# A three-part decoder block on one core: the memory turned by VectorE and stored in the first phase, instead of turned by TensorE in the second

## The reference, cut to what matters

```
x = x + attn(layernorm(x))             # linear attention, 16 heads, conv with 3 taps, projections Wq Wk Wv Wp
x = x + xattn(layernorm(x), ctx_1024)  # cross-attention on a memory of 512 x 512 per batch
x = x + ffn(layernorm(x))              # a gated recurrence over the 16 batches, then tanh

xattn: mn = mem * rsqrt(mean(mem^2) + 1e-6) * (1 + rms_scale)   # one factor per memory row, one per feature
       k, v = mn @ kv_w[0], mn @ kv_w[1]                        # 1 key/value head of 128
       q    = rmsnorm(x) @ q_w                                  # 4 query heads of 128
       k, q = rope(k), rope(q);  softmax(q k^T, masked) v;  @ out_w
```

## Time and profile before

| | |
|---|---|
| median of 3 runs | 3089.86 us (3088.77 to 3090.32) |
| the profiled execution | 3088.35 us |
| its span | 3086.6 us |
| granted TensorE clock, mean | 0.996 |
| PE busy | 3034.9 us, 98% |
| DVE, ACT, POOL busy | 61%, 41%, 27% |
| HBM read and written | 184.57 MB, 98.57 MB |

### The profile page before, as it was taken

One profiled execution on the slowest core, in us unless ns is written; L12 is line 12 of the kernel. 1 busy time (PEld: TensorE's weight loads), 2 busy tenths in 40 slices (PEclk: granted clock), 3 DMA queues, 4 the chain that ended last, 5 costly groups with the idle time before them and its releaser, 6 DMA issues.

```text
span 3086.6 us, 40196 instructions
## 1 busy us (share of the span) xinstructions
PE 3034.9 (98%) x15108; PEld 2557.7 (83%) x15108; DVE 1894.2 (61%) x4081; ACT 1272.5 (41%) x2419; POOL 828.9 (27%) x699
## 2 busy tenths in 40 slices
PE   8999999999889999999999989999999999999999
PEld 7888888888768888888888878888888888888887
DVE  6777777778588777877877765243233343332455
ACT  4434343434366666666666653122211221212243
POOL 0101010111146666766666650000000000000144
PEclk9999999999999999999999999999999999999999
DMA  4555555554621122212221232111211112111386
GB/s 150 140 148 139 150 137 156 131 161 126 191 78 65 61 71 82 71 56 84 69 71 56 82 110 65 59 51 52 62 41 41 41 55 55 55 28 45 138 291 225
DMA packets 232385, 300.42 MB, mean 97 GB/s; under 512 B 13056, under 2 KB 111360, under 8 KB 232192
## 3 DMA queue, kind: packets, MB, share of 16 engines
q1 hardware_dynamic: 232192, 297.85, 31.8%
HBM read 184.57 MB, written 98.57 MB: 92 GB/s over the span
## 4 chain that ended last, share of the span: by engine, by line
PE 96%; DVE 2%; issue 1%; ACT 1%; DMA 1%; POOL 0%; SPq 0%; DVEq 0%; ACTq 0%
PE c_p L131 11%; PE c_p L132 11%; PE c_p L130 11%; PE a_p L130 6%; PE a_p L132 6%; PE a_p L131 6%; PE b_n L132 5%; PE b_n L130 5%; PE b_n L131 5%; PE b_t L1663 3%; PE d_p L131 2%; PE d_p L130 2%; PE d_p L132 2%; PE a_r L130 2%; PE a_r L131 2%; PE a_r L132 2%
## 5 line engine op out<-in xcount | busy, mean ns | idle before, releaser
L1283 POOL TENSOR_SCALAR b_soft<-b_soft,b_one_in_sum 128x512 f32<-128x512 f32 x256 | 401.2, 1568 | 299.9 <-DVE b_one_in_sum L1466 299.9
L1912 ACT ACTIVATE c_gate<-c_p,c_bias 128x512 f32<-128x512 f32 x180 | 124.2, 690 | 682.6 <-PE c_p L132 682.6
L1942 DVE TENSOR_TENSOR c_gate<-c_gate,c_gate 128x512 f32<-128x512 f32 x64 | 44.2, 690 | 503.1 <-ACT c_gate L1912 503.1
L1485 DVE TENSOR_TENSOR b_p_lo<-b_t,b_p_hi 128x512 fp32r<-128x512 f32 x256 | 175.1, 684 | 159.2 <-ACT b_p_hi L1340 156.5
L1331 ACT ACTIVATE b_soft<-b_soft,b_minus_top 128x512 f32<-128x512 f32 x256 | 185.2, 724 | 180.6 <-DVE b_minus_top L1477 176.0
L351 POOL TENSOR_TENSOR kept_scale<-c_ln_ve,minus_half 128x4 f32<-128x4 f32 x16 | 16.1, 1009 | 880.0 <-DVE c_ln_ve L343 880.0
L1340 ACT ACTIVATE b_p_hi<-b_t 128x512 fp32r<-128x512 f32 x256 | 151.6, 592 | 107.9 <-PE b_t L1663 107.9
L616 ACT ACTIVATE a_elu<-a_p 128x512 f32<-128x512 f32 x128 | 75.5, 590 | 284.5 <-PE a_p L132 284.5
L351 POOL TENSOR_TENSOR a_ln_sc<-a_ln_ve,minus_half 128x4 f32<-128x4 f32 x16 | 16.3, 1018 | 627.2 <-DVE a_ln_ve L343 627.2
L1477 DVE CUSTOM_DVE_ANT_0 b_soft<-b_l,b_mask_row 128x512 f32<-128x512 f32 x256 | 175.2, 685 | 0.0
L1663 PE MATMUL b_t<-ident,b_soft 128*128 128x128 f32 x1024 | 154.8, 274 | 10.9 <-DVE b_p_lo L1485 9.8
(11 more groups left out here) (294 smaller groups left out, 9572.9 us busy)
## 6 DMA issues: line engine op xcount, KB each, us to landing
a_res<-in_x SPq DMA_DIRECT2D x16, 1024.0 KB, 6.8
a_att_shuffled<-x SPq DMA_DIRECT2D x64, 256.0 KB, 5.1
x<-a_res SPq DMA_DIRECT2D x16, 1024.0 KB, 5.2
b_mem<-in_ctx SPq DMA_DIRECT2D x16, 1024.0 KB, 5.4
b_x<-x SPq DMA_DIRECT2D x16, 1024.0 KB, 5.5
b_res<-x SPq DMA_DIRECT2D x16, 1024.0 KB, 5.5
x<-b_res SPq DMA_DIRECT2D x16, 1024.0 KB, 4.5
c_x<-x SPq DMA_DIRECT2D x16, 1024.0 KB, 5.5
```

Source lines behind the costliest of these rows:

```text
L1283: pool.tensor_scalar(soft[:, at, :], soft[:, at, :], one_in_sum[:, at:at + 1], None, ALU.mult).then_inc(p_norm.sem, p_norm.unit)
L1485: dve.tensor_tensor(part.low, pT_bank[:, :].rearrange("p (i s) -> p i s", i=T), part.high_f32(), ALU.subtract).then_inc(p_lo.sem, p_lo.unit)
L1912: act.activation(gate[j % 2][i][:, :], gating.banks[(3 * j + i) % 6][:, :], ACT.Tanh if g == "c" else ACT.Sigmoid, bias=added[:, i, j:j + ...
```

## The change

- **Phase A, every step.** The memory of the batch is loaded twice (`load_memory`, behind the stores of the step before): in token rows into `mem_turned` and shuffled into `mem_moving`. ACT squares the token rows with a sum per row (`memory_square`, behind `elu_front(3)` and ahead of `values(0)`). DVE then overwrites `mem_turned` with the turned memory (`memory_turned`, behind `weight_low(WP)`, ahead of its wait for `att_moved`). SP stores it to the scratch tensor x2 (`store_memory`).
- **To make room**, tokens and attention results are shuffled into the buffers they came from (`x`, `att`) and both go through x1.
- **Phase A's end.** The attention result of the last batch isn't sent through DRAM: PE turns it (`turn_last`), between the first products of phase B, into one PSUM bank.
- **Phase B.** `turn_memory`, `square` and `mem_apply` are gone. `load_mem` loads the turned memory, in the contiguous direction, into `memT_f`, the place of the low part. It now waits for the key/value products of `new`, and stands behind `load_x`. ACT copies the high part in slots 6 to 9, POOL subtracts the low part in slots 7 to 10. The factors of all 16 x 512 memory rows are made at once on POOL at the end of A (`mem_power`, 128x64). They are applied in `values_high` (four 128x128 copies with a scale for each half, instead of one of 128x256) and in `keys`.
- Feature order in phase B is interleaved (feature = 4 p + c), so weights are loaded as `(p c)` and x is turned with `turn_interleaved` (a step of 16 B between elements).

```diff
@@ phase A: SP, then DVE
+            def load_memory(sp, b):
+                if b >= 1:
+                    sp.wait_ge(mem_stored.sem, mem_stored.upto(b - 1))
+                self.load_shuffled(sp, mem_moving, io["ctx_1024"], b, mem_in)
+                sp.dma_start(mem_turned[:, :, :], self.token_rows(io["ctx_1024"], b)).then_inc(mem_in.sem, mem_in.unit)
+            def store_memory(sp, b):
+                sp.wait_ge(mem_squared.sem, mem_squared.upto(b))
+                sp.dma_start(self.token_rows(self.x2, b), mem_turned[:, :, :]).then_inc(mem_stored.sem, mem_stored.unit)
+            def memory_turned(dve, b):
+                dve.wait_ge(mem_sq.sem, mem_sq.upto(b))
+                for c in range(C):
+                    self.turn_squares(dve, mem_turned, mem_moving, c).then_inc(mem_squared.sem, mem_squared.unit)
...
@@ PE, called in phase B's step 0: c = 0 in slot 0, the others in slot 2
+            def turn_last(pe, c):
+                if c == 0:
+                    pe.wait_ge(*last_bank_freed)
+                    pe.wait_ge(att_sb.sem, att_sb.upto(B - 1))
+                else:
+                    pe.wait_ge(z_f.sem, z_f.upto(B - 1, c - 1))
+                self.turn_interleaved(pe, last_bank, att, c).then_inc(attT.sem, attT.unit)
...
@@ phase B: SP, ACT, POOL
             def load_mem(sp, b):
                 if b >= 1:
-                    sp.wait_ge(memT_ps.sem, memT_ps.upto(b - 1))
-                sp.dma_start(mem[:, :, :], self.token_rows(io["ctx_1024"], b)).then_inc(mem_in.sem, mem_in.unit)
+                    sp.wait_ge(kv_ps.sem, kv_ps.upto(b - 1))
+                sp.dma_start(memT_f[:, :, :], self.token_rows(self.x2, b)).then_inc(mem_in.sem, mem_in.unit)
...
+            def memory_high(act, b, c):
+                act.wait_ge(mem_in.sem, mem_in.upto(b))
+                act.activation(memT.high[:, c, :], memT_f[:, c, :], ACT.Copy).then_inc(mem_hi.sem, mem_hi.unit)
+            def memory_low(pool, b, c):
+                pool.wait_ge(mem_hi.sem, mem_hi.upto(b, c))
+                pool.tensor_tensor(memT.low[:, c, :], memT_f[:, c, :], memT[:, c, :].high_f32(), ALU.subtract).then_inc(mem_lo.sem, mem_lo.unit)
...
@@ a step of phase B on SP
                     if following(new, B):
-                        load_mem(sp, new.b + 1)
                         load_mask(sp, new.b + 1)
                         load_x(sp, new.b + 1)
+                        load_mem(sp, new.b + 1)
...
@@ on POOL
+                        if following(new, B) and 7 <= j <= 10:
+                            memory_low(pool, new.b + 1, j - 7)
...
@@ on ACT
                         if old and j < J - 2:
                             exp(old.b, j + 2)
...
-                            if 3 <= j <= 6:
-                                square(act, after, j - 3)
-                            if j == 8:
-                                mem_apply(act, after, 0)
-                                mem_apply(act, after, 1)
-                            if j == 10 or j == 11:
-                                mem_apply(act, after, j - 8)
+                        if after and 6 <= j <= 9:
+                            memory_high(act, after, j - 6)
...
@@ on PE
-                        if following(new, B) and j in (13, 14):
-                            turn_memory(pe, s, new.b + 1, 2 * (j - 13))
-                            turn_memory(pe, s, new.b + 1, 2 * (j - 13) + 1)
```

More of the change, by code:

```diff
@@ L535, in phase_a @@
             ATT, OUT = 0, GROUPS
+            last_bank, last_bank_freed = first.bank(B, 1), first.freed(B, 1)
             raw_bank = lambda i, c: second.banks[(C * i + c) % 3]
@@ L549, in step @@
                         sp.dma_start(res[:, :, :], self.token_rows(io["x"], old.b)).then_inc(res_in.sem, res_in.unit)
-                    if old:
+                    if new and old:
                         shuffle_att(sp, old.b)
@@ L565, in step @@
                         self.b_load_query_weight(sp)
+                    if new:
+                        store_memory(sp, new.b)
+                    if following(new, B):
+                        load_memory(sp, new.b + 1)
+                    if new and new.b == B - 1:
                         sp.wait_ge(kq_ps.sem, kq_ps.upto(B - 1))
                         self.b_load_memory_weight(sp)
+                        sp.wait_ge(mem_stored.sem, mem_stored.upto(B - 1))
+                        self.b_load_output_weight(sp)
                         sp.wait_ge(kv_ps.sem, kv_ps.upto(B - 1))
@@ L596, in step @@
                     if new and new.b == B - 1:
-                        self.b_mem_power(pool, 0)
+                        self.b_mem_power(pool)
+                        for c in range(C):
+                            self.b_memory_low(pool, 0, c)
                 pipeline(B, step)
@@ L647, in step @@
                         weight_high(WQ, 2)
+                        for t in range(T):
+                            memory_square(act, new.b, t)
                     for c in range(C):
@@ L682, in step @@
                             self.b_memory_weight_high(act, c)
+                        for c in range(C):
+                            self.b_memory_high(act, 0, c)
                 def tokens_high(b, c):
@@ L798, in step @@
                         weight_low(WP, 2)
+                        memory_turned(dve, new.b)
                     if old:
@@ L1012, in phase_b @@
             p = [self.split(ctx, f"b_p{i}", [P, T, S]) for i in range(2)]
-            mem = sb("mem", [P, T, D])
+            memT = Split(sb("memT_hi", [P, C, S], F32R), Place(nc, self.base + 1024 * 196).tile("b_memT_lo", [P, C, S], F32R))
+            memT_f = Place(nc, self.base + 1024 * 196).tile("b_memT_f", [P, C, S])
             rope = sb("rope", [P, 4, S])
@@ L1303, in step @@
                             query_low(old.b, 3)
-                        if j == 7 and following(new, B):
-                            mem_power(pool, new.b + 1)
                         if new:
@@ L1424, in step @@
                             tokens_high(j - 4)
-                        if after and j >= 14:
-                            memory_high(act, s, after, 2 * (j - 14))
-                            memory_high(act, s, after, 2 * (j - 14) + 1)
                         if old and j < J - 2:
@@ L1547, in step @@
                             p_low(fin.b, J - 1)
-                        if after and j == 15:
-                            memory_low(dve, s, after, 2)
-                            memory_low(dve, s, after, 3)
                         if old and j < J - 2:
@@ L1732, in step @@
                             keys_values(1)
+                            if s == 0:
+                                for c in range(1, C):
+                                    self.a_last_turn(pe, c)
                         if 3 <= j <= 6:
```

185 lines of the change are left out of this document (79 added, 106 removed).

## The result

The changed kernel takes 3196.6 us (median of four runs, 3193.1 to 3198.1), the kernel before took 3089.3 beside it: ratio 1.0345, interval 1.0328 to 1.0361. It is slower by 107 us; the forecast was 67.5 slower. The profiled execution has a span of 3194.7 us against 3086.6, +108.1.

What follows compares the result with a forecast made beforehand. PE, busy 98% of the span and all of 100 us in mid-phase B, was taken as the bound. Terms -26 - 17.5 + 90 + 21 = +67.5 on 3088.35 gave 3155.9, as a median 3157 us; range 3118 to 3182.

Steps and rivals of the forecast that it cites:

- Removed from PE: Phase B, batches 1 to 15: 60 groups of memory turns at 0.44 us each leave PE, 26 us gained.
- End of A: End of phase A: PE turns the last attention result itself, so x's turns come earlier; 17.5 us gained, ends 10 and 20.
- Late load: Phase B: memory load behind load_x stalls PE before turn_p(7), 5.9 us in steps 1 to 14, 7.5 in step 0; +90.
- Clock: Phase B, behind the stalls: most end at 1.2 GHz, 1.4 us lost each, 15 times; +21, ends 0 and 42.
- Phase A: Steps of A: DVE's four extra transposes, 4.15 us, fill its wait for the attention result; 0, at worst 31.
- Small edits and strided turns: Phase B: POOL's and ACT's edits stay off the path, at worst 15 us; 16 B turns at most 1 us; both taken 0.
- lower end of the term: Late load in phase B: if memory lands 5.4 us after its own issue, the stall is 3.7 us, all in all 55.
- uncut upper end: Whole time with the upper ends of wait and clock: 3089.9 - 36 + 100 + 42 = 3196, before cutting to 3182.
- A: Rival for phase B: only the turns count, ACT's wait for the memory is covered; 3046 us, chance 9%.
- B: Rival for phase B: the stall comes but the clock holds; 3136 us, chance 25%.
- C: Rival: VectorE becomes the bound of phase A too, as the hole closes and the 2.1 us slack is used; 3188 us, 7%.

Runs made afterwards that it cites:

- e4: e1 with two groups of four memory turns put back on PE in slot 14, into a bank nobody reads; 3079.7 us.
- e8: e1 with exp(15) behind p_high(13) on ACT and the reciprocal for tile 15 behind masked on DVE; 3076.9 us.
- e11: e8 with POOL's scale for x behind tile 0's scaling in slot 15, and DVE normalising x's first part behind p_lo(15) in slot 0; 3071.1 us.
- e2: Changed kernel with ACT's copy of the memory in slots 7 to 10 and POOL's subtraction in slots 8 to 11; 3151.9 us.
- e10: e1 with the first memory's five loads behind the second x, and POOL's bias additions at A's end behind DVE's last z_lo; 3076.2 us.
- e9: e1 with x turned in contiguous pieces instead of every fourth word, so results differ from the reference; 3075.6 us.
- e1: Changed kernel with load_mem issued ahead of load_x in phase B; 3080.4 us, ratio to before 0.9972.
- e7: Changed kernel with the products of encode(old, 0) done three times instead of once in slot 7; 3171.2 us.
- e12: e11 with the first memory's loads behind the second x, and POOL's bias additions at A's end behind DVE's normalised x; 3064.4 us, ratio to before 0.9920.

## Why the prediction was wrong in size

Direction and main mechanism were right; the time was 40 us too low and outside the range. By its own steps, in the profiled executions (the sums are over all steps of B, slot by slot against before):

| Step of the prediction | forecast | measured | from |
|---|---|---|---|
| Removed from PE | -26 | -7.7 | slots 13 to 15: 7.92 to 7.36, steps 1 to 14; no gain seen in step 0 |
| End of A | -17.5 | -13.6 | b_x issue -9.23 with +4.35 of the start in it |
| Late load | +90 | +88.9 | slot 7 of steps 1 to 14, 81.4 in sum (5.8 each), + 7.50 |
| Clock | +21 | +27.4 | slot 8 of steps 1 to 14, 26.1 in sum (1.9 each), + 1.3 in step 0 |
| Phase A | 0 | +4.4 | stores of x1 |
| Small edits and strided turns | 0 | +8.6 | slots 0 to 6: +0.57 in each of 13 steps; step 15 and behind it +1.2 |
| Sum | +67.5 | +108.0 | the spans differ by 108.1 |

**The late load: right.** Place, victim and length (5.9 and 7.5 forecast; 4.84 to 5.91, 5.6 on average, and 7.50 measured), the two issues within 0.4 us, ACT's wait of 9.4 (I said 8 to 9), PE busy for 93 of 100 (I said 91). That step 0 fits to the hundredth is luck: its own terms, 10.2 - 2.5, give 7.7. (The lower end of the term, given as 55, comes to 57 in the same way.)

**Removed from PE: the step that failed.** It said that "each operation taken from it is a gain of its length", from a PE that shows 100%. In slot 13 the turns gave 0.70 of their 0.87 us, in slot 14 nothing, and slot 15 grew by 0.15. The loop of handovers between DVE and ACT that the turns had covered holds 2.68 us a slot, and e4 shows it by putting eight turns back for nothing. Two handovers in a row bounded it: e8 cut this loop, and only with the next one cut too (e11) did the step follow PE's own work. My check of the next handover was made in slots 6 and 7 only, whereas the turns stood in 13 and 14, the two slots with the least other work. The sentence that I wrote myself there, that a full PE "says nothing about how near the other engines' handovers are", applied to the removal first of all. I also named no range for this term, so that its miss of 18.3 us, the largest of all, was outside any bound.

**The clock: right in kind, low in size.** 1.9 a stall instead of 1.4. The reason I gave for the fall, a stall "longer than 4.6", was worth nothing: in e2 it fell behind ten stalls of 1.98 to 3.77 us, and held behind three, of 2.17, 2.20 and 3.62. As I took the time at half speed (2.8 us) from one place at the end of A, so I had one sample; in the step above the clock is low from before 1260 until about 1265.8, 3.6 us after PE starts at 1262.24, and half of that is 1.8. The Trainium skill ("TensorE: Matmul & The Clock Gate", section "HAM oscillation — how this bites in real kernels") says that a wait for a DMA in each round of a loop throttles anew in each round; all 14 steps of the changed kernel agree.

**Phase A.** Its steady steps are as forecast: DVE's transposes fit into the hole and PE stays at 100. What I left out was the first step, where five DMAs stand ahead of the second x while SP's issues are slow (8.68 us for four). For B the prediction asked what stands ahead of a load in SP's list; here it did not. e10 shows it: with the five behind that load the wait is gone.

**End of A.** The chain came as told, but each low part took 1.03 to 1.38 us instead of the 0.69 that I had from a stretch in which POOL was idle. The power over 128x64 took 10.5 us (I estimated 17), hidden as expected.

**Small terms.** Strided turns at 0 were wrong by 0.23 a step (e9); 0.35 a step, most of it in slot 3, is not traced to a cause. All misses but one went the same way, which a range from single ends could not hold. The uncut upper end, 3196, meets the measured time by luck: it was made of a longer load and a dearer clock, neither of which came.

**The rivals.** A named the gain that e1 shows to be there (3080), but valued the turns at full length, 3046. B is excluded by the windows and by e7. C is excluded: phase A's steps did not grow.

## What to carry to other kernels

A load's place in its queue is set by the waits ahead of it: before moving one, write down when it is issued, when it lands, and which in-order engine asks for it first; here two lines in the other order were 116 us. Before crediting a removed operation on a full engine with its length, go to the very slots where it stands and sum the loop of handovers there without it, or look for a step of the same kernel that does without the operation, as step 15 here: the engine's idle share shows only what the removed work did not cover. And when a loop is cut and the step does not move, look for the engine that now waits longest just behind; cutting only both loops gave the 0.66 us a step.

## What was not expected of the hardware

- A stall of TensorE of 1.98 us was enough for the granted clock to fall, and one of 3.62 was not (e2: it fell in ten steps of thirteen); a stall of 5.9 filled with products kept it at 1.00 in e7's full steps. Each fall cost 1.8 us in e7's comparison of slot 8.
- VectorE slowed beside GpSimd, by operation: subtraction of two SBUF inputs 0.68 alone, 1.03 to 1.38 beside it; normalisation in place (one SBUF input, fp32) 0.48 alone, 1.19 beside it; `k_swap`, a product of two SBUF inputs of 128 columns, 0.28 alone and 1.36 to 1.38 beside it (e12). GpSimd's additions took 1.26 each alone, 1.32 to 1.59 beside these. The Trainium skill ("SBUF — State Buffer", section "Who interferes with whom") says that a VectorE instruction with two SBUF inputs contends with a GpSimd instruction that reads SBUF. The subtractions and `k_swap` agree: they lost 0.35 to 1.1 us each, the most where the operation itself is shortest. The same section says that VectorE in a two-port mode, which a tensor_scalar can enter, contends with GpSimd, and that the one that comes second is fully blocked while the other's instruction lasts. The normalisations are such operations and lost 0.7 us each on average beside additions of 1.43; whether each of them was blocked, and for how long, no run here shows.
- A weight load for a turn takes 140 ns from contiguous words (e9) and 204 with a stride of 16 B (e1, medians); of the 64 ns difference 0.23 / 16 = 14 ns a turn showed in the step.
- SyncE's issues took 8.68 us for four DMAs of 256 KB while the first loads were under way, against 1.91 to 2.96 for the same four in the later steps (1.93 or less in eleven of fifteen).
